# Graph attention with a sorted staircase: r placed by a factorized one-hot, c grouped by counts and a scan

## The reference

```python
XW = X @ W                                   # X: 2048 x 128
s_col, s_row = XW @ a[0, :f], XW @ a[0, f:]
Z1  = leaky_relu(s_row[:, None] + s_col[None, :], 0.01)
den = exp(Z1)                                # 2048 x 2048
num = A @ den                                # A: 2048 x 2048
att = where(num != 0, den / num, 0)
H   = A @ (att @ XW)
out = layernorm(X + H)
```

## Time and profile before

| | |
|---|---|
| median of 3 runs | 464.31 us (463.53 to 465.45) |
| span of the profiled execution, first to last instruction | 463.2 us |
| PE busy | 331.5 us (72%) |
| DVE busy | 317.1 us (68%) |
| ACT busy | 198.6 us (43%) |
| POOL busy | 188.3 us (41%) |
| mean granted TensorE clock | 0.839 of 2.4 GHz |

### The profile page before, as it was taken

The page is one execution under the profiler, slowest core; times in us unless marked ns, Lnnn a source line. Parts: engine busy times, 40 slices in busy tenths (PEclk is TensorE's granted clock), DMA queues, the critical chain, the costliest instruction groups (busy, mean ns, idle before and its releaser), DMA issues.

```text
span 463.2 us, 7133 instructions
## 1 busy us (share of the span) xinstructions
PE 331.5 (72%) x2214; PEld 166.9 (36%) x2215; DVE 317.1 (68%) x497; ACT 198.6 (43%) x308; POOL 188.3 (41%) x164
## 2 busy tenths in 40 slices
PE   4853718759784333579999999999999840399960
PEld 2553614435561111224343444433444320144420
DVE  0579989998938673869898999975999900201026
ACT  1110022123313474668777777766777840100010
POOL 4000024355555788557454544642556457000000
PEclk9875555697998569689999999999999985599995
DMA  3030043435552325500000000000000041300002
GB/s 111 0 92 2 3 139 95 131 99 178 183 178 74 102 69 150 156 1 0 2 1 0 0 0 0 0 0 0 0 0 0 1 123 52 96 1 0 0 24 68
DMA packets 13877, 24.68 MB, mean 53 GB/s; under 512 B 2080, under 2 KB 8608, under 8 KB 13728
## 3 DMA queue, kind: packets, MB, share of 16 engines
q0 software_dynamic: 5632, 18.88, 13.4%
q1 hardware_dynamic: 8224, 5.51, 4.1%
HBM read 21.23 MB, written 3.15 MB: 53 GB/s over the span
## 4 chain that ended last, share of the span: by engine, by line
PE 50%; DVE 24%; POOL 10%; issue 5%; DMA 5%; ACT 3%; POOLq 0%; SPq 0%; DVEq 0%; ACTq 0%
PE ps L395 17%; PE ps L364 12%; PE ps L424 9%; DVE D L573 5%; DVE D L575 4%; POOL xws L249 3%; POOL d_b L277 3%; PE ps L390 3%; DMA stage<-adjT,perm 3%; PE ps L354 2%; DVE Alo L728 2%; DVE D L579 2%; POOL Alo L233 2%; DVE xws L576 2%; POOL stage L223 2%
## 5 line engine op out<-in xcount | busy, mean ns | idle before, releaser
L267 POOL TENSOR_TENSOR crow<-rrow,cj 128x512 f32<-128x512 f32 x64 | 79.3, 1239 | 79.0 <-DVE crow L751 77.7
L395 PE MATMUL ps<-Ahi,D 128*128 x248 | 87.2, 382 | 2.9 <-issue 1.4
L354 PE MATMUL ps<-Ahi,E 128*96 128x512 f16 x128 | 57.1, 499 | 44.5 <-POOL Alo L233 25.2
L223 POOL DMA_INDIRECT stage<-adjT,perm x32 | 38.9, 1216 | 101.2 <-DVE rs L599 54.6
L754 DVE TENSOR_TENSOR tmp<-crow,tmp 128x512 f32<-128x512 f32 x64 | 65.4, 1022 | 18.3 <-ACT tmp L503 16.5
L364 PE MATMUL ps<-stage,xwp 128*128 128x512 f32 x128 | 71.6, 641 | 2.4 <-DVE stage L741 2.4
L448 ACT CAST Ahi<-stage 128x1024 f16<-128x1024 f32 x32 | 33.2, 1045 | 62.7 <-DMA stage<-adjT,perm 62.2
L424 PE MATMUL ps<-Ahi,D 128*128 128x512 f16 x128 | 40.2, 393 | 24.0 <-DVE D L766 24.0
L501 ACT ACTIVATE tmp<-ps 128x512 f32<-128x512 f32 x64 | 38.1, 595 | 37.7 <-PE ps L397 37.7
L751 DVE SCALAR_TENSOR_TENSOR crow<-crow 128x512 f32<-128x512 f32 x64 | 49.5, 773 | 0.0
L395 PE MATMUL ps<-Alo,D 128*128 x124 | 47.2, 380 | 0.0
(11 more groups left out here) (137 smaller groups left out, 445.5 us busy)
## 6 DMA issues: line engine op xcount, KB each, us to landing
tmp<-xT SPq DMA_DIRECT2D x1, 1024.0 KB, 4.8
d_xw<-stage SPq DMA_DIRECT2D x1, 1024.0 KB, 5.1
xws<-d_b SPq DMA_DIRECT2D x2, 512.0 KB, 4.8
out<-crow SPq DMA_DIRECT2D x4, 256.0 KB, 2.3
stage<-adjT,perm POOLq DMA_INDIRECT x32
xws<-d_xw,perm POOLq DMA_INDIRECT x16
d_b<-crow,ranku POOLq DMA_INDIRECT x16
stage<-wT SPq DMA_DIRECT2D x1, 64.0 KB, 1.9
```

What stands on the lines that cost most here:

```text
L223: nc.gpsimd.indirect_dma_start(out=st[n % NG], out_offset=None, in_=rows, in_offset=bass.IndirectOffsetOnAxis(ap=perm[:, 0, h, b:b + 1], a ...
L267: nc.gpsimd.tensor_tensor(q_t[c % 2], rrow[:, c * W:(c + 1) * W], cj[:, u:u + 1].to_broadcast([P, W]), ALU.add).then_inc(S["q_ready"], 1)
L354: mm = nc.tensor.matmul(ps[0:R, c, :], E[:, e, b, :], a[:, b, c * W:(c + 1) * W], start=(b == 0 and i == 0), stop=(b == NB - 1 and i == 2))
L395: nc.tensor.matmul(num[c], D[:, d, bass.ds(slot, 1), :], a[:, bass.ds(k, 1), c * W:(c + 1) * W], start=False, stop=(i == 2), skip_group_ch ...
```

## The change

r's ranks are found as before. A rank is then split into its high four and low seven bits. `highhot` marks the block, multiplied with the five values (`moved`, 16 x 5 x 16 elements), `lowhot` marks the place in it (16 operations of 128), and 16 matmuls of 80 columns do what 16 x 16 did. c is no longer ranked. `grp` counts for each element of c the blocks of r whose largest value doesn't exceed -c; `hot` marks the group. Two matmuls count the elements of a group before an element in the same column (`less`; tri - 1 has the sign turned) and in whole columns (`ones16`), `tensor_tensor_scan` adds these up, and the place in order of groups comes out; within a group c stays unsorted. The same function then places c. All this stands before iteration 0; the placing matmuls come at PE's iteration 1, `fetch_places` at DVE's 2, the copy to `crow` at 4, xws one per iteration from 6, the staircase at 8 and 9, its weights and batches 12 iterations earlier too. Its bounds come from the scan's counts, without `d_rs`.

```diff
-STAIR = NB + 4
+CROW = 4
+STAIR = 8
+XWG = 6
...
-        def c_steps(n):
...
-            sp.wait_ge(S["perm_r"], 1)
-            sp.dma_start(d_rs, rs[:, :]).then_inc(S["rs_out"], 16)
-            sp.wait_ge(S["rs_out"], 16)
-            sp.dma_start(ends[:, 0, :], d_rs[0:1, :].to_broadcast([P, NB])).then_inc(S["ends_in"], 16)
-            sp.dma_start(ends[:, 1, :], d_rs[P - 1:P, :].to_broadcast([P, NB])).then_inc(S["ends_in"], 16)
...
-                if n == NB + 2:
+                if n == XWG:
                     pool.wait_ge(S["perm_c"], 1)
-                if NB + 2 <= n < NB + 2 + NB // 2:
+                if XWG <= n < XWG + NB:
...
-                    for b in range(2 * (n - NB - 2), 2 * (n - NB - 1)):
+                    for b in range(n - XWG, n - XWG + 1):
...
+            def place_sorted(i):
+
+                pe.wait_ge(S["hots"], i + 1)
+                for b in range(NB):
+                    mm = nc.tensor.matmul(bt[1][:, 0:5 * NB], lowhot[:, b, :], moved[:, b, :, :].rearrange("p v h -> p (v h)"),
+                                          start=(b == 0), stop=(b == NB - 1))
+                mm.then_inc(S["p_place"], 1)
+
+            place_sorted(0)
+            pe.wait_ge(S["perm_r"], 1)
+            nc.tensor.matmul(bt[0][:, 0:NB], onesr[0:1, :], rs[0:1, :], start=True, stop=True).then_inc(S["thr"], 1)
+            pe.wait_ge(S["hot"], 1)
+            nc.tensor.matmul(bt[2][:, 0:NB * NB], less[:, :], hot[:, :], start=True, stop=True)
+            nc.tensor.matmul(bt[3][:, 0:NB * NB], ones16[:, :], hot[:, :], start=True, stop=True).then_inc(S["p_pre"], 1)
             pe.wait_ge(S["xw_sb"], 1)
             for n in range(2 * NB):
-                for step in c_steps(n):
-                    sort_step(1, step)
-                if n == NB + 2:
+                if n == 1:
+                    place_sorted(1)
+                if n == CROW:
...
-                if n == NB + 2:
+                if n == CROW:
+                    act.wait_ge(S["cmax"], 1)
                     act.wait_ge(S["crow_t"], 1)
...
+            def mark_places(i, at):
+
+                link(V.tensor_scalar(split[:, 1, :], at, P - 1, None, ALU.bitwise_and))
+                link(V.tensor_scalar(split[:, 0, :], at, 7, None, ALU.logical_shift_right))
+                link(V.tensor_copy(place[:, :, :], split[:, :, :]))
+                link(V.tensor_tensor(highhot, place[:, 0, :].unsqueeze(2).to_broadcast([P, NB, NB]),
+                                     ramp16[:, 0:NB].unsqueeze(1).to_broadcast([P, NB, NB]), ALU.is_equal))
+                V.tensor_tensor(moved, highhot.unsqueeze(2).to_broadcast([P, NB, 5, NB]),
+                                vals[:, i, :, :].unsqueeze(3).to_broadcast([P, NB, 5, NB]), ALU.mult)
+                for b in range(NB):
+                    op = V.tensor_scalar(lowhot[:, b, :], ramp16[:, 0:P], place[:, 1, b:b + 1], None, ALU.is_equal)
+                op.then_inc(S["hots"], 1)
...
-            for step in range(2 * NB):
-                if step == NB:
-                    fetch_ranks(0)
-                sort_step(0, rrow, rcol, step)
-            fetch_places(0, rs, "perm_r")
-
-            link(V.tensor_reduce(sc[:, 7:8], rrow[:, :], AX.X, ALU.max))
...
+            for b in range(NB):
+                rank_step(b)
...
             V.tensor_copy(ccol[:, :], bt[2][:, 0:W:W // NB]).then_inc(S["ccol_sb"], 1)
+            V.tensor_reduce(sc[:, 2:3], crow[:, :], AX.X, ALU.max).then_inc(S["cmax"], 1)
+            dve.wait_ge(S["flags_used"], NB)
+            link(V.tensor_copy(ranku[:, :], bt[0][:, 0:NB]))
+            mark_places(0, ranku[:, :])
+            fetch_places(0, rs, "perm_r")
+
             dve.wait_ge(S["ccol_sb"], 1)
             values(1, ccol)
+            dve.wait_ge(S["thr"], 1)
+            link(V.tensor_copy(sc[:, 7:8], bt[0][:, 0:1]))
...
+            link(V.tensor_tensor(cmp3, ccol[:, :].unsqueeze(2).to_broadcast([P, NB, NB]),
+                                 bt[0][:, 0:NB].unsqueeze(1).to_broadcast([P, NB, NB]), ALU.add))
+            link(V.tensor_scalar(cmp3, cmp3, 0.0, None, ALU.is_le))
+            link(V.tensor_reduce(grp[:, :], cmp3, AX.X, ALU.add))
+            link(V.tensor_scalar(grp[:, :], grp[:, :], float(NB - 1), None, ALU.min))
+            V.tensor_tensor(hot3, grp[:, :].unsqueeze(1).to_broadcast([P, NB, NB]),
+                            ramp16[:, 0:NB].unsqueeze(2).to_broadcast([P, NB, NB]), ALU.is_equal).then_inc(S["hot"], 1)
+
+            dve.wait_ge(S["p_pre"], 1)
+            link(V.tensor_tensor_scan(incl[:, :], onesr[:, 0:1].to_broadcast([P, NB * NB]), bt[3][:, 0:NB * NB], 0.0, ALU.mult, ALU.add))
+            link(V.tensor_tensor(spread, incl[:, :], bt[2][:, 0:NB * NB], ALU.add))
+            link(V.tensor_tensor(spread, spread, hot, ALU.mult))
+            link(V.tensor_reduce(rank[:, 1, :], spread.rearrange("p (m j) -> p j m", m=NB), AX.X, ALU.add))
+            link(V.tensor_copy(split[:, 0, :], rank[:, 1, :]))
+            mark_places(1, split[:, 0, :])
...
-                for o, (re, ce, op) in enumerate(((rmin, cmin, ALU.is_gt), (rmax, cmax, ALU.is_le))):
-                    link(V.tensor_tensor(jk3, ce.unsqueeze(2).to_broadcast([P, NB, NB]), re.unsqueeze(1).to_broadcast([P, NB, NB]), ALU.add))
-                    link(V.tensor_scalar(jk3, jk3, 0.0, None, op))
-                    link(V.tensor_reduce(t16[:, o, :], jk3, AX.X, ALU.add))
+                upto = incl[:, NB - 1:NB * NB:NB]
+                for o in range(2):
+                    at = cstt[:, 4 + NB + NS + o * NB:4 + NB + NS + (o + 1) * NB]
+                    link(V.tensor_tensor(jk3, upto.unsqueeze(1).to_broadcast([P, NB, NB]), at.unsqueeze(2).to_broadcast([P, NB, NB]), ALU.is_le))
+                    link(V.tensor_reduce(t16[:, 1 - o, :], jk3, AX.X, ALU.add))
...
             for n in range(2 * NB):
-                if n == NB // 2:
-                    fetch_ranks(1)
-                for step in c_steps(n):
-                    sort_step(1, crow, ccol, step)
-                if n == NB + 1:
+                if n == 2:
                     fetch_places(1, cs, "perm_c")
```

More of the change, by code:

```diff
@@ L92, in graph_attention_layernorm @@
         xwp = sb("xwp", [P, 2, FEAT])
-        ends = sb("ends", [P, 2, NB])
+        split = sb("split", [P, 2, NB], U32)
+        incl = sb("incl", [P, NB * NB])
+        place = sb("place", [P, 2, NB])
+        grp = sb("grp", [P, NB])
         sc = sb("sc", [P, 8])
@@ L118, in graph_attention_layernorm @@
         idt = xws[:, 768:768 + 2 * NB].rearrange("p (b v) -> p b v", v=2)
-        flags = [D[:, :, :, :].rearrange("p a s j -> p (a s j)")[:, i * N:(i + 1) * N].bitcast(BF16) for i in range(3)]
+        less = xws[:, 800:864].bitcast(BF16)
+        ones16 = xws[:, 864:928].bitcast(BF16)
+        cmp3 = xws[:, 1024:1024 + NB * NB].rearrange("p (j b) -> p j b", j=NB)
+        spread = xws[:, 1536:1536 + NB * NB]
+        onesr = xws[:, 1792:1792 + P]
+        flags = [D[:, :, :, :].rearrange("p a s j -> p (a s j)")[:, i * N:(i + 1) * N].bitcast(BF16) for i in range(3)]
+        lowhot = flags[0].rearrange("p (b j) -> p b j", b=NB)
+        hot = flags[2][:, 0:NB * NB]
+        hot3 = hot.rearrange("p (m j) -> p m j", m=NB)
+        highhot = flags[2][:, NB * NB:2 * NB * NB].rearrange("p (b h) -> p b h", b=NB)
+        moved = flags[1][:, 0:NB * 5 * NB].rearrange("p (b v h) -> p b v h", b=NB, v=5)
         ramp16 = wgt
@@ L334, in _ @@
-            pe.wait_ge(S["const"], 5)
-            for step in range(2 * NB):
-                sort_step(0, step)
+            pe.wait_ge(S["const"], 5)
+            for b in range(NB):
+                fl = flags[b % 3]
+                pe.wait_ge(S["flags"], b + 1)
+                for kb in range(NB):
+                    nc.tensor.matmul(bt[0][:, kb:kb + 1], fl[:, kb * P:(kb + 1) * P], onesb[:, :],
+                                     start=(b == 0 and kb == 0), stop=(b == NB - 1), skip_group_check=True)
+                nc.tensor.matmul(bt[0][:, b:b + 1], tie[:, b % 3, :], onesb[:, :], start=False, stop=(b == NB - 1),
+                                 skip_group_check=True).then_inc(S["flags_used"], 1)
@@ L581, in fetch_ranks, with rank_step @@
-            def fetch_ranks(i):
-                dve.wait_ge(S["flags_used"], i * 2 * NB + NB)
-                if i == 0:
-                    link(V.tensor_copy(ranku[:, :], bt[0][:, 0:NB]))
-                V.tensor_copy(rank[:, i, :], bt[0][:, 0:NB]).then_inc(S["ranked_sb"], 1)
-                dve.wait_ge(S["ranked_sb"], i + 1)
+            def rank_step(b):
+                if b >= 3:
+                    dve.wait_ge(S["flags_used"], b - 2)
+                fl = flags[b % 3]
+                v = rcol[:, b:b + 1]
+                m = (b + 1) * P
+                V.tensor_scalar(fl[:, 0:m], rrow[:, 0:m], v, None, ALU.is_lt)
+                if m < N:
+                    V.tensor_scalar(fl[:, m:N], rrow[:, m:N], v, None, ALU.is_le)
```

(23 more changed lines are left out.)

63 lines of the change are left out of this document (12 added, 51 removed).

## The result

The changed kernel took 448.72 us, the median of 4 runs (446.65 to 450.06), against 464.07 us before in the same comparison: ratio 0.965, 95% interval 0.9615 to 0.9683. Forecast was 445.5 us. Run once more with the experiments it took 448.61 us, ratio 0.967 (0.962 to 0.973).

The account below looks back on a forecast made before the run. DVE, filled by c's sort, was taken to bound the fetch stage until the sort is done. No gain to cast 5, then 113.4 - 94.6 = 18.8 off 463.2 gives 444.4, plus 1.1: 445.5 us; range 440 to 451, chance 0.57.

Parts of the forecast that it names:

- r's part: Ranking and placing r before the fetch stage: r stands sorted at 57.5 us, 2.7 earlier than before.
- c's part: DVE's work on c before the first subtraction: E filled at 70.7 us against 65.7 before, 5 us later.
- No gain by gather 5: Start of the fetch stage: gather 5 issued behind 79.1 us (79.01 before), cast 5 at about 83.5 in both kernels.
- crow's copy: ACT's copy behind cast 4 waits for PE's transposes: 4.88 idle + 1.86 = 6.7 us; casts 5 and later queue behind it.
- The 26 half-blocks: Rest of the fetch stage after cast 5: 94.6 us instead of 113.4, a gain of 18.8.
- The xws calls: POOL's gathers, one per half-block from 6 to 21: 0.53 us each, 13 outside stalls, 6.9 us.
- plain pace: Fetch ring with three buffers: 2.7 us per half-block, taken between 2.3 and 3.76; 26 x 2.7 = 70.2 us.
- The check over the last 13 half-blocks of before: Same terms applied to the old kernel where no sort was left: 63.9 us, measured 64.6.
- The ring: Rival for the fetch stage: POOL's calls shorten too, pace 2.35, 9 us less, 436 us; chance 0.17.
- transfers: Rival: three gathers in flight share the engines, pace stays 3.0 to 3.3, 453 to 461 us; chance 0.21.
- the rival for a slowdown: xws calls in POOL's queue ahead of gathers: 475 us if all like the longest, deciding from 2.1 us each; chance 0.04.
- One sign of being wrong: In the fetch stage, the forecast would be wrong if POOL is busy throughout 6 to 21.

Follow-up runs that it names:

- experiment 5: Changed kernel with PE's 16 matmuls that place c ahead of half-block 0's sums instead of behind them: 446.61 us, ratio 0.962 to the kernel before.
- experiment 6: Changed kernel with ACT's copy of crow behind cast 6 instead of cast 4: 443.71 us, ratio 0.954 to the kernel before.
- experiment 4: Changed kernel without xws gathers on POOL; one plain transfer on SP's queue brings XW in natural order: 441.16 us, ratio 0.950 to the kernel before.
- experiment 10: Changed kernel with all subtractions on DVE and four stage buffers instead of three: 433.06 us, ratio 0.932 to the kernel before.
- experiment 2: Changed kernel, but c still ranked by 16 whole-row comparisons in iterations 0 to 7, then placed by factorized one-hot: 459.85 us, ratio 0.991 to the kernel before.
- experiment 1: Kernel before with only r placed by the factorized one-hot; c's ranking and one-hots stay in iterations 0 to 16: 459.60 us, ratio 0.991.
- 3: Changed kernel with other work at its old places (crow at 18, xws two per iteration from 18, staircase at 20): 448.48 us, ratio 0.965 to the kernel before.
- after: The changed kernel itself, about 448.7 us.
- experiment 7: Changed kernel with all 32 subtractions on DVE, none on POOL: 435.15 us, ratio 0.938 to the kernel before.

## Why the prediction was right

**r's part.** r stood sorted at 57.34 us (forecast 57.5). The run's start was 0.8 us later than before's (last tie 46.85 against 46.09), so the chain itself was 1.0 shorter than worked out: 16 lowhots took 2.69 (2.9), moved 1.49 and 1.41 to the next start (1.4), PE's matmuls and their wake-up 1.34 (1.8).

**c's part.** E was full at 70.9 (70.7). The scan took 0.69 us; I took 0.6. The Trainium skill's half throughput (DVE: opcode table, instruction layouts, handler registers and perf-mode slots, section Datapath and trigger behaviour) had led to about 0.7, and this trace agrees: 0.42 us for other operations of 256 elements, 0.69 for the scan.

**No gain by gather 5.** It was issued at 78.91 (79.1; before 79.01). This reading is right as far as it goes, but cast 5 was not free to follow at 83.5, as the forecast's own term for crow's copy had it. One bound beside it was worked out wrong: with moved 1.0 and the lowhots 1.3 cheaper for each vector, the lower prices give about 4.6 us, not 3.

**The 26 half-blocks.** From 83.5 to 181.3 is 97.8 us, forecast 94.6. By terms: at crow's copy ACT waited and copied for 8.3 + 1.9 = 10.2 us, not 6.7, because PE's transposes now come behind subtraction and sums of half-block 3 and took 4.9 us at a mean granted clock of 0.86 (78 to 90 us; 3.73 us at 1.00 in experiment 5). But that idle time is not the cost: cast 5 stood 7.2 us behind 83.5, cast 8 (98.32) 6.7 behind 83.5 and three turns of 2.7, and moving the copy gave back 5.0 (experiment 6). The term held. The staircase cost less, 5.4 + 2.1 instead of the 10.3 before buffers give back (ACT's idle time after cast 9 was 5.4 us, not 8 to 11). The weights' waits were 2.3 + 1.5 = 3.8, as forecast. The xws calls cost 7.5 (6.9, experiment 4). The plain pace of 2.7 stood for a ring in which POOL's subtraction is one turn in four; without xws it was 2.77 (experiment 4), with the last xws calls 3.03. The 3.2 us came after cast 10. Its terms give 3.58 us a turn for casts 10 to 21 (2.7, 0.53 for the xws call, and 3.8 for the weights over 11 turns), measured 3.71, and 2.86 for casts 21 to 31, measured 3.03. The check over the last 13 half-blocks of before, which bore 2.7 out, was worth more than the derivation from latencies (2.3).

**Time around the span.** The profiled run took 446.65 us with a span of 444.9, so 1.75 us lie around the span. I took 1.1. The forecast's span, 444.4, hit the trace by luck of the run: its cast 31 came 3.2 us later than the forecast's 178.1 and its last part was 2.7 shorter than before's. The spans of the four runs had a median of 446.95. That and the 0.65 us are the 3.2 by which 445.5 was short.

**The rivals.** The ring did not come to its floor: the gathers' calls shortened in the median (976 ns, 1186 before) but hardly in the mean (1.16 us, 1.22 before), and casts 25 to 31, without xws calls, were 2.89 us apart. Nor was it held up by transfers, as experiment 10 shows. The pace above 2.7 came at least in part from POOL's queue, which I had as the rival for a slowdown with calls of 2.1 us. The xws calls had a median of 0.95 us and a mean of 1.15, the longest 1.84. Their number was enough to make the queue the bound. One sign of being wrong that the forecast named was nearly there: from iteration 6's xws call at 96.7 us to iteration 21's at 158.3 POOL waited for DVE once, 2.8 us. So the forecast was right about what DVE's relief is worth, and too kind to POOL: it left 0.72 us a turn free where the trace from 138 to 152 us shows none.

**What the change is worth by parts.** r's placing: 4.8 us alone, of which the maximum over crow in front of it takes about 2 back. Factorized placing of c by itself, as experiment 2 places it: nothing (1 against 2). Moving the other work forward: nothing (3). Grouping c in place of ranking and placing it: the rest, some 11 us (459.6 and 459.85 against 448.5). It takes about 33 us of comparisons and the wide one-hots off DVE. In return E is full at 70.9 us, against 61.0 in experiment 1 and 60.4 in experiment 2. The wide one-hots that go with it cost about 3 us of time (8 x 0.34 to 0.42).

## What to carry to other kernels

When an engine that releases buffers loses a third of its work (DVE from 60 us to the last cast: 108.9 us busy before, 75.1 after), ask at once which queue is next: here it was POOL, with two issues and a quarter of a subtraction per turn, and handing that subtraction to the engine just relieved was worth nearly as much (13.5 us) as the whole rewrite (15.4). Price a piece of the old work by the pace of the loop with and without it, not by its busy time: a pair of ranking steps took some 4 us of DVE and cost 1.4. And in a queue that runs in order, place a copy that waits for another engine behind the work that waits for nothing: two iterations later gave 5 us.

## What the hardware showed that was not expected

A DVE operation on 16 elements took 2.66 us. DVE, then POOL, of the kernel after:

```profile
97.19 2.66 DVE L681 TENSOR_SCALAR t<-t 128x16 f32<-128x16 f32 x1
```

```profile
97.68 2.13 POOL L235 TENSOR_TENSOR Alo<-stage,Ahi 128x1024 f16<-128x1024 f32 x1
```

It ended at 99.85 us, as POOL's subtraction did (99.81); the same operation takes 0.17 us elsewhere. The Trainium skill (SBUF — State Buffer, section SBUF: two separate sides) calls the port pair that the two engines share an exclusive lock, held for a whole instruction; the end of this row agrees with it, for an operation of 16 elements too. Its start does not settle who came first: DVE's row begins 0.5 us before POOL's, when POOL was still issuing an xws gather (96.71 to 97.66). With POOL's subtractions gone (experiment 7) the same line took 0.17 us.

Single slices of 0.5 us moved up to 442 GB/s with four stage buffers (experiment 10) and up to 393 with three (experiment 7, 140 to 160 us), where after averaged 101 to 186 GB/s over the three stretches of 30 us from 90 to 180 us: in these runs the rate of this stage is set by who issues and who frees buffers, not by the transfers.
